# Second attention: distance products in two 64-column array tiles, and 96 of 128 query rows in the distance and probability transfers

## The reference, cut to what matters

```python
H, D, TEXT, IMG, MAXREL = 16, 64, 77, 16, 16
q = heads(x @ Wq)                                  # 128 query rows per batch
sim = einsum('bihd,bjhd->bhij', q, k) * SCALE      # k from 77 text rows
dist = clip(arange(TEXT)[None, :] - arange(nq)[:, None], -MAXREL, MAXREL) + MAXREL
sim = sim + einsum('bihd,ijd->bhij', q, rel_k[dist]) * SCALE
attn = softmax(sim)
out = attn @ v + einsum('bhij,ijd->bihd', attn, rel_v[dist])
out = out + stream(image rows) + stream(audio rows)   # two more softmax attentions
x = x + out @ Wo + bo
```

## Time and profile before

| | before |
|---|---|
| median of 3 runs | 996.1 us (995.76 to 1000.56) |
| span of the profiled execution | 992.7 us |
| PE, DVE, ACT, POOL busy | 90%, 62%, 47%, 38% of the span |
| second attention | about 453 to 875 us of the span |
| mean granted TensorE clock | 0.962 |

### The profile page before, as it was taken

One profiled execution on the slowest core, in us unless ns is written; L12 is line 12 of the kernel. 1 busy time (PEld: TensorE's weight loads), 2 busy tenths in 40 slices (PEclk: granted clock), 3 DMA queues, 4 the chain that ended last, 5 costly groups with the idle time before them and its releaser, 6 DMA issues. The chain is left out here.

```text
span 992.7 us, 26217 instructions
## 1 busy us (share of the span) xinstructions
PE 891.3 (90%) x8784; PEld 758.1 (76%) x8785; DVE 612.0 (62%) x1561; ACT 469.1 (47%) x1209; POOL 379.8 (38%) x555
## 2 busy tenths in 40 slices
PE   4888889777999999997999899999999999779995
PEld 3677667636999999995556598888888887667784
DVE  3588788754455555542017466768667686549895
ACT  3777777712222222221333444445444454349895
POOL 4477677530000000006101446445464444426762
PEclk9998999987999999998999999999999999879998
DMA  4454447432433333315765798897989986411121
GB/s 119 145 164 145 143 148 237 140 145 94 128 108 93 98 93 108 93 44 181 262 225 180 165 188 185 179 182 164 200 172 176 172 178 150 90 33 55 60 61 49
DMA packets 222059, 137.78 MB, mean 139 GB/s; under 512 B 160289, under 2 KB 207393, under 8 KB 221857
## 3 DMA queue, kind: packets, MB, share of 16 engines
q1 hardware_dynamic: 180304, 99.78, 40.1%
q10 hardware_dynamic: 38608, 28.64, 10.8%
q0 software_dynamic: 3072, 8.39, 2.6%
HBM read 81.79 MB, written 54.98 MB: 138 GB/s over the span
## 5 line engine op out<-in xcount | busy, mean ns | idle before, releaser
L1717 ACT ACTIVATE c_pT<-c_T 128x512 f32<-128x512 f32 (+2 forms) x90 | 50.2, 595 | 104.4 <-PE c_T L1876 73.3
L1666 POOL TENSOR_TENSOR c_soft<-c_soft,c_share 128x616 f32<-128x616 f32 (+2 forms) x96 | 70.3, 760 | 63.4 <-DVE c_share L2129 61.8
L1062 ACT ACTIVATE b_rowsT<-b_RT 128x256 f32<-128x256 f32 x39 | 15.0, 383 | 158.2 <-PE b_RT L1104 158.2
L1173 DVE COPY b_w<-moe_w 128x1024 f32 x78 | 53.5, 687 | 56.2 <-issue 50.7
L1676 POOL MEMSET d_round<- 128x1 f32 x1 | 0.1, 98 | 226.5 <-POOLq L953 226.5
L1113 PEld LDWEIGHTS b_G<-b_rowsT,b_w 128*128 128x128 f32 x624 | 77.2, 195 | 4.2 <-DVE b_w L1173 1.5
L1113 PE MATMUL b_G<-b_rowsT,b_w 128*128 128x128 f32 x624 | 77.9, 279 | 1.5 <-ACT b_rowsT L1062 1.3
L1113 PE MATMUL b_U<-b_rowsT,b_w 128*128 128x128 f32 x624 | 76.1, 275 | 0.0
L1187 DVE SCALAR_TENSOR_TENSOR b_hidT<-b_U,b_bias,b_gate 128x128 f32<-128x128 f32 x156 | 43.9, 343 | 51.9 <-PE b_U L1113 45.4
L1140 PE MATMUL b_Y<-moe_w,b_hidT 128*128 x312 | 73.9, 380 | 0.9 <-DVE b_out L1218 0.9
L1113 PEld LDWEIGHTS b_U<-b_rowsT,b_w 128*128 128x128 f32 x624 | 72.9, 192 | 0.0
(11 more groups left out here) (231 smaller groups left out, 2167.2 us busy)
## 6 DMA issues: line engine op xcount, KB each, us to landing
rel_windows<-c_relw ACTq DMA_DIRECT2D x28, 368.0 KB, 6.7
c_bias<-rel_windows SPq DMA_DIRECT2D x16, 616.0 KB, 5.6
prob_rows<-c_soft SPq DMA_DIRECT2D x16, 616.0 KB, 7.3
moe_w<-in_L_Wl SPq DMA_DIRECT2D x16, 512.0 KB, 4.1
early<-in_L_early SPq DMA_DIRECT2D x16, 384.0 KB, 3.2
values<-c_pT ACTq DMA_DIRECT2D x22, 256.0 KB, 3.8
b_rows<-expert_lists SPq DMA_DIRECT2D x39, 128.0 KB, 2.0
expert_out<-b_out SPq DMA_DIRECT2D x39, 128.0 KB, 1.7
```

What stands on the lines that cost most here:

```text
L1173: nc.vector.tensor_copy(own[p][h][:, :, :], w1[:, bass.ds(e, 1), :, h * HE:(h + 1) * HE].rearrange("p o c n -> p (o c) n"))\
L1666: ins = nc.gpsimd.tensor_tensor(soft[p][:, hs, a:z], soft[p][:, hs, a:z], share[:, s, hs].unsqueeze(2).to_broadcast([P, HS, z - a]), ALU.mult)
L1717: nc.scalar.activation(dst, view(T[k]), ACT.Copy, **kw).then_inc(g["emptied"], 1)
```

## The change

The distance products, 8 per batch with all 128 columns of the array (128 rows of `qT`: two heads by 64 of depth, and 128 queries as columns), become 16 with 64 columns each, one for queries 0 to 63 and one for queries 64 to 127, in two column tiles. The moving operand is the same `relk` with 64 columns. The DMAs of the windows, the bias, the probabilities and the band carry 96 of 128 query rows (`NEAR` is 96). The last 32 rows of `bias` and `band` are set to zero once by POOL in the prologue, over the whole tiles, behind a new semaphore `s_far`, for which SP waits ahead of the first `rel_in`; the clearing of `bias` waits until PE has used the text context in it. `band_values` streams 96 columns of `bandT` in place of 128. POOL's `tails`, DVE's work and ACT's copies stay at 128 rows.

```diff
+NEAR = -(-(TEXT + MAXREL - 1) // 16) * 16
...
-                sp.dma_start(bias[p][:, :, :], sheared(rel_d[p], P - 1, -1, P, TEXT)).then_inc(s_relin[p], 16)
+                sp.dma_start(bias[p][0:NEAR, :, :], sheared(rel_d[p], P - 1, -1, NEAR, TEXT)).then_inc(s_relin[p], 16)
...
-                sp.dma_start(prob_d[p][:, :, MAXREL:MAXREL + TEXT], soft[p][:, :, 0:TEXT]).then_inc(s_pout[p], 16)
+                sp.dma_start(prob_d[p][0:NEAR, :, MAXREL:MAXREL + TEXT], soft[p][0:NEAR, :, 0:TEXT]).then_inc(s_pout[p], 16)
...
-                sp.dma_start(band[p][:, :, 0:NSTEP - 1], sheared(prob_d[p], 1, 1, P, NSTEP - 1)).then_inc(s_pin[p], 16)
+                sp.dma_start(band[p][0:NEAR, :, 0:NSTEP - 1], sheared(prob_d[p], 1, 1, NEAR, NSTEP - 1)).then_inc(s_pin[p], 16)
...
+            sp.wait_ge(s_far, 4)
             for q in two:
                 rel_in(q, 0, q)
...
+            for p in two:
+                nc.gpsimd.memset(band[p][:, :, :], 0.0).then_inc(s_far, 1)
+            pool.wait_ge(g["filled"], 2 * MT1 + 2 * (TEXT_TILES - EARLY_TILES))
+            for p in two:
+                nc.gpsimd.memset(bias[p][:, :, :], 0.0).then_inc(s_far, 1)
             pool.wait_ge(s_folded, 1)
...
-                    act.dma_start(rel_d[p][:, h * HS:(h + 1) * HS, at:RELW], w[:, :, at:RELW]).then_inc(s_relout[h], 16)
+                    act.dma_start(rel_d[p][0:NEAR, h * HS:(h + 1) * HS, at:RELW], w[0:NEAR, :, at:RELW]).then_inc(s_relout[h], 16)
...
-                    for j in range(MS):
-                        ins = nc.tensor.matmul(bank[:, j * 2 * NSTEP:(j + 1) * 2 * NSTEP], qT[p][:, u * MS + j, :], relk[:, :],
-                                               start=True, stop=True)
+                    for j, a in itertools.product(range(MS), two):
+                        half = slice(a * DH1, (a + 1) * DH1)
+                        ins = nc.tensor.matmul(bank[half, j * 2 * NSTEP:(j + 1) * 2 * NSTEP], qT[p][:, u * MS + j, half], relk[:, :],
+                                               start=True, stop=True, tile_position=(0, a * DH1))
...
-                            ins = nc.tensor.matmul(O[u][a * DH1:(a + 1) * DH1, q, :], steps_v[r, :], bandT[r, q, :],
+                            ins = nc.tensor.matmul(O[u][a * DH1:(a + 1) * DH1, q, 0:NEAR], steps_v[r, :], bandT[r, q, 0:NEAR],
```

More of the change, by code:

```diff
@@ L1476, in attention1 @@
         s_clear = sem("c_clear")
+        s_far = sem("c_far_rows")
         s_steps = sem("c_rel_steps")
```

## The result

The changed kernel takes 985.89 us (median of 4 runs, 983.11 to 987.42) against 996.25 us for the kernel before beside it. The ratio is 0.9889, with an interval of 0.9867 to 0.991: faster by 1.1%. The forecast was 986.7 us, in a range of 981 to 994. The profiled execution took 986.18 us with a span of 984.3 us, so 1.9 us lie around the span (1.8 to 2.1 in every execution of which both numbers are known) and not the 3.4 us that I had carried over. So the profiled execution of the kernel before, with its span of 992.7 us, was itself some 1.5 us shorter than the median of its runs.

A forecast was written before the change was run, and what follows sets the result against it. PE was taken to bound long intervals, DVE and POOL's `far` the short ones. Long intervals 5.6, written-out short ones 0.4, start 1.85 and end 1.55 sum to 9.4 us off 996.1: 986.7 us, range 981 to 994.

The forecast's parts named there:

- Long intervals: Between output sums where PE makes keys for two batches: PE-bound, 0.94 us less in each of six, 5.6 us.
- Short intervals: The other intervals between output sums: POOL's `far` holds DVE's subtraction, so 18.24 us stays; gain 0 in the loop's four.
- the signs that were named: Short intervals: subtraction about 2.2 us, ending 0.66 behind `far`; PE's wait for `xn` up to 1.6; loop clock 1.00.
- Rival B: Short intervals: DVE's subtraction is late by itself, so they gain too; 14.7 us less, 981.4; chance 0.1.
- two written-out short intervals: Short intervals in batches written out rather than looped: 0.2 us each, between 0 and 0.94.
- C: Distance products: both tiles' loads share one way in, a pair costs 0.11, no gain there; 993.5 us; chance 0.12.
- D: Distance products: a tile's load waits for the other tile's streaming matmul, 3.4 us; slower, about 1017 us; chance 0.05.
- Rival E: Loop: PE's longer wait for `xn` lowers the granted clock and eats the long intervals' gain; about 996 us; chance 0.08.
- The start: Ahead of the first output sum: 0.95 us from step 1, 0.9 from step 0 and two prologue batches.
- The clearing: POOL's zeroing in the prologue: estimated 3.2 us of work, costing 0 us, with 5 us of cover.
- The end: Block's end: 1.4 us from probabilities and band DMAs, 1.55 with the last band products; 0 for the two steps before.
- Around the span: Whole kernel: median lies 3.4 us above the profiled span, so 983.3 of span becomes 986.7 us.

The follow-up runs named there:

- e4: Changed kernel with POOL's `far` product on one of 16 heads per batch: 985.38 us, ratio 0.9832 to the kernel before.
- e5: Changed kernel with DVE subtracting the maximum from the two image parts (PSUM) first, the text part last: 982.45 us, ratio 0.988 to the kernel before.
- e6: Changed kernel with POOL making half of `far` right behind each half's normalising: 983.82 us, ratio 0.988 to the kernel before.
- e3: Changed kernel with each group's four distance products of tile 0 first, then four of tile 1: 993.35 us, ratio 0.9931 to the kernel before.
- e1: Kernel before with only the two-tile distance products; transfers and band products stay at 128 rows: 996.66 us against 999.27, ratio 0.9966.
- e2: Changed kernel with the old distance products, so 96 rows in transfers and band products alone: 994.66 us against 999.27 for the kernel before, ratio 0.9931.
- e8: Changed kernel again, unchanged, as the measure for e5 to e7: 986.67 us, ratio 0.9928 to the kernel before.
- e11: Changed kernel once more, unchanged, beside e9: 987.34 us, ratio 0.9909 to the kernel before.
- e9: Changed kernel with `far` in halves as in e6, but in the last two batches behind both normalisings: 979.45 us, ratio 0.9829 to the kernel before.
- e7: Changed kernel with both `far` in halves and DVE's text part last: 985.73 us, ratio 0.9901 to the kernel before.

## Why the prediction was right, point by point

**Long intervals: right, mis-sized by 0.08.** Forecast 0.94 us each, measured 1.01 to 1.05. The distances gave 0.82 (forecast 0.8), the band products 0.21 (forecast 0.15): I had counted 7 distances at the products' stream, and the group gives about a fifth, 0.21 of 1.03, for a quarter less of columns. Six give 6.2 and not 5.6.

**Short intervals: right, and shown.** 0 was forecast, in the profile after it is 0.0, with the signs that were named: L2125 stretched (2.35 us, forecast 2.2), 0.66 us behind `far`, the wait of PE's load queue for `xn` 1.53 us (up to 1.6), the clock at 1.00. POOL ends `far` 17.13 us behind the output sum where it did at 17.10, so its chain was indeed not shortened. Rival B is refuted by 18.26. The two written-out short intervals gave 0.3 together (forecast 0.4, which was an even choice between 0 and 0.94). That POOL's `far` is the cause, and not a companion, rests on e4 (17.12 with a short `far`), on e5 (only the part that reads SBUF is held) and on e6 (when DVE's instruction is first, POOL's is the one stretched). In every run with a stretched subtraction, which is every run but e4, its end is 0.65 or 0.66 us behind the end of the POOL instruction that was running when it became ready, wherever that was. The Trainium skill, "SBUF — State Buffer" (Terms), has it that VectorE and GpSimd arbitrate for one SBUF port pair, and that whoever holds it keeps it for the whole instruction while the other is fully blocked. By that rule DVE must wait for the end of a POOL instruction and not run slower beside it; the trace agrees, in the 0.66 that don't depend on how long the wait was (0.31 to 1.91 us in before).

**Rivals C and D: refuted.** A pair of loads costs neither 0.11 nor waits for the other tile's stream: 32 matmul records pass in 1.11 us, 0.035 each, where by D they would take 3.4 in all. In PE's load queue the loads of the two tiles start 0.007 us apart and the next pair 0.05 to 0.06 later, as I had read it from `weighted`. The rule of the Trainium skill, "TensorE: Matmul & The Clock Gate", Part 3, that loads overlap matmuls in flight only across row groups, does not hold for two column tiles in the same row group here. e3 shows that the order counts, with 0.36 us a batch.

**Rival E: refuted for the loop.** In the three profiles of the changed kernel the clock is 1.00 from 610 to 810. It falls near both ends of the block, before too. In kind the rival did come true outside the loop: in e1 it fell from 604.0 to 607.4, behind a wait of PE of 2.06 us, and that interval took 20.57 us.

**The start:** 1.85 forecast, 1.98 in the first profile, but 4.9 and 0.6 in the two others: right by luck or not, it can't be told. The groups of the two prologue batches and of step 0 take 1.44 us where they took 1.96, so 0.5 each and not 0.3; the second half of a group waits 0.2 us for ACT, as forecast in kind. The clearing cost nothing: 1.01 and 2.19 us, 3.2 together as estimated, and the first `rel_in` was issued at 517.00.

**The end: the step that was wrong, in size and in place.** "I take 1.4" for the two DMAs, with 0.15 for the products, and 0 for the steps ahead of them. The last three intervals gave 0.95, and all of it came ahead of those DMAs. Two rows of the kernel before, beside those of the changed kernel above, show it:

```profile
841.57 0.60 SPq L1559 DMA_DIRECT2D prob_rows<-c_soft  x1
...
845.45 1.42 DVE L2135 TENSOR_REDUCE c_band<-c_far 128x16 f32<-128x1232 f32 x1
```

From the output sum that opens the last three intervals to the second-last `prob_out` it is 12.06 us before and 12.07 after. From there to the last `prob_out` it is 15.19 (841.57 to 856.76) and 14.24 (833.16 to 847.40), 0.95 less. From the last `prob_out` to the last output sum it is 16.40 in both. The 0.95 came from the subtraction. Before, it began 0.46 us behind the start of `far` (842.08 and 841.62), was held, and DVE came to `ends` 3.88 us behind `prob_out`. After, it began at 832.98, ahead of `far`, so that `far` was the one that was held (2.83 us for 2.37), and `ends` came 2.91 us behind `prob_out`. All that follows on DVE, up to the last probabilities, was earlier by that. So the mechanism that I had named for the short intervals worked here too, at a place that I had put at 0.

The change alone would not have turned that order. Counted from the same output sum, PE starts these scores at 8.10 us where it did at 8.31, the 0.21 of the band products, and that is less than the 0.46 missing. The rest is the clock: before, it was at 0.5 from 838.0 to 841.4, over these scores (1.91 us for 1.16), and after the change it was not low there. e2 shows the two apart: there the scores start at 8.10 too, but the clock is at 0.5 from 840.2 to 843.6, the subtraction is held for 2.65 us, and the two `prob_out` stand 15.21 us apart, as before. So the gain of the last three intervals hangs on where the half-clock stretch lies, and what puts it there no run shows.

Behind the last `prob_out` the DMAs did get shorter. From its issue to the landing of the band it is 8.23 us in the profile after (7.63 and 7.83 in e8 and e11) where it was 8.90, so 0.7 to 1.3 less and not 1.4. Where PE has nothing to do, that shows as time: 8.30 us to `bands` in e2 (1.33 us idle) and 7.75 in e9 (839.82 to 847.57, 2.31 us idle) against 8.99. In the changed kernel none of it arrived: PE, at half clock from 841.6 to 851.9, spent 6.76 us on the second-last output product (5.34 before) and became the last to be ready.

**Around the span, and the luck in the number:** 3.4 us carried over, 1.9 in this execution. The sum by span was 983.3 and 984.3 was measured. By terms, the long intervals gave 0.6 us more than forecast, the start 0.1 more in this profile, the end 0.6 less, the written-out intervals 0.1 less, and the part behind the last output sum, which I had left alone, took 0.9 back. That the median came within 0.8 us is partly these errors against each other, and partly the 3.4.

## What to carry to other kernels

Read for each kind of interval which instruction ends last and what that one waits for, before you multiply a gain by all intervals: here the same 1.03 us counted six times of twelve. Where an SBUF-only instruction of VectorE is longer than its usual duration, compare its end with the end of a GpSimd instruction; if they are tied, cut or order GpSimd's work so that VectorE's stands ready at a boundary, and expect a step, not a slope (0.07 us late cost 0.67, by e7 beside e6). A gain in a drained tail, where PE has no work of later batches left to fill its waits, is worth what the slowest of PE, at whatever clock it has there, and the DMAs leaves.

## What the runs showed that I had not expected

The boundary between two GpSimd instructions decides by hundredths: 17.12 in e6 and 17.79 in e7 differ by when DVE was ready, 0.51 us ahead of the start of the second half of `far` or 0.07 behind it. Two column tiles in alternation bring the 16 products of a batch (32 loads) through in 1.11 us, and in blocks by tile in 1.47, less than the 1.8 of loads one after the other. The one subtraction that slipped ahead of `far` at the end of the block, with the clock at full level there, gave 0.95 us, nearly as much as a long interval, where a quarter less data in the transfers behind it gave nothing. In the drained tail the stretches in which TensorE's granted clock is 0.5 lie elsewhere in nearly every kernel (838 to 841 and 852 to 859 before, 842 to 852 after the change, 821 to 825 and 849 to 855 in e9), while the three profiles of the changed kernel agree. The last three intervals ranged from 41.9 (e5) to 46.5 us (e1), 4.6 us, where the change gives 6.2 in the six long intervals; how much of that range is the clock's wasn't taken apart.
